# Reordering the opening of an attention and expert kernel: where transposes, scores, the projections of the values and a weight copy stand

## The reference

```python
def xattn(x, y):                                   # x normalized, y = ctx
    q = (x @ Wq + bq).reshape(B, N, 16, 32)
    k = (y @ Wk + bk).reshape(B, 77, 16, 32)
    v = (y @ Wv + bv).reshape(B, 77, 16, 32)
    attn = softmax(einsum('bnhd,bmhd->bhnm', q, k) / sqrt(32))
    out = einsum('bhnm,bmhd->bnhd', attn, v).reshape(B, N, 512)
    return relu(out @ W1 + b1) @ W2 + b2           # 512 -> 1024 -> 512
x = x + xattn(layernorm(x), ctx)
x = x + ffn(layernorm(x))                          # 8 experts, top-1 by layernorm(x) @ Wg.T
```

## Time and profile before

| | |
|---|---|
| median of 3 runs | 1497.59 us (1496.52 to 1498.39) |
| the profiled execution | 1497.29 us |
| its span, first to last instruction | 1495.4 us |
| granted TensorE clock, mean | 0.992 |
| TensorE busy (matmul) | 1462.3 us, 98% |
| VectorE, ScalarE, GpSimd busy | 1028.6, 721.8, 423.4 us |

### The profile page before, as it was taken

The page is one execution under the profiler, slowest core; times in us unless marked ns, Lnnn a source line. Parts: engine busy times, 40 slices in busy tenths (PEclk is TensorE's granted clock), DMA queues, the critical chain, the costliest instruction groups (busy, mean ns, idle before and its releaser), DMA issues.

```text
span 1495.4 us, 23924 instructions
## 1 busy us (share of the span) xinstructions
PE 1462.3 (98%) x7764; PEld 1219.5 (82%) x7764; DVE 1028.6 (69%) x2524; ACT 721.8 (48%) x2026; POOL 423.4 (28%) x312
## 2 busy tenths in 40 slices
PE   7899999999999999999999999999999999999998
PEld 5678787888888888878787888888888878778996
DVE  5666667586868586777767686757585757558665
ACT  5455454453536353635454453536353535434553
POOL 1342121203122222222121203121222222127776
PEclk9899999999999999999999999999999999999999
DMA  7130110213020303131211201120202011649873
GB/s 286 37 101 1 50 36 20 71 44 104 22 99 1 106 15 93 39 84 44 70 51 37 85 22 57 42 89 1 85 1 85 1 57 57 210 172 286 252 236 113
DMA packets 70445, 122.05 MB, mean 82 GB/s; under 512 B 21871, under 2 KB 30336, under 8 KB 69302
## 3 DMA queue, kind: packets, MB, share of 16 engines
q1 hardware_dynamic: 59526, 86.83, 19.4%
q0 software_dynamic: 10800, 33.70, 5.9%
HBM read 75.61 MB, written 46.40 MB: 82 GB/s over the span
## 4 chain that ended last, share of the span: by engine, by line
PE 94%; DVE 3%; ACT 1%; issue 1%; DMA 0%; POOL 0%; POOLq 0%; SPq 0%; DVEq 0%; ACTq 0%
PE bank L1176 24%; PE bank L1198 24%; PE bank L991 11%; PE bank L1128 8%; PE bank L1017 7%; PE bank L1092 4%; PE bank L1600 4%; PE bank L1644 4%; PE bank L1267 2%; PE bank L1583 2%; PE bank L959 2%; PE bank L1245 1%; DVE actH L1109 1%; ACT actH L1103 1%; PE bank L850 1%
## 5 line engine op out<-in xcount | busy, mean ns | idle before, releaser
L1176 PE MATMUL bank<-actA,w 128*128 128x512 f32 x1536 | 373.2, 396 | 2.1 <-issue 2.1
L1198 PE MATMUL bank<-w,actH 128*128 128x512 f32 x1536 | 372.1, 393 | 0.0
L1176 PEld LDWEIGHTS bank<-actA,w 128*128 128x128 f32 x1536 | 285.8, 189 | 64.5 <-issue 2.4
L1198 PEld LDWEIGHTS bank<-w,actH 128*128 128x128 f32 x1536 | 283.0, 188 | 55.9
L1086 POOL TENSOR_TENSOR E<-E,rc 128x1232 f32<-128x1232 f32 x64 | 144.7, 2261 | 460.5 <-DVE rc L1080 460.5
L1342 POOL DMA_INDIRECT region<-rows,pos x64 | 63.8, 997 | 456.4 <-DVE pos L1336 417.9
L991 PE MATMUL bank<-actA,wq 128*128 128x512 f32 x768 | 182.8, 390 | 0.0
L1183 ACT ACTIVATE actH<-bank,b 128x512 fp32r<-128x512 f32 x128 | 88.4, 690 | 190.4 <-PE bank L1176 190.4
L1059 ACT ACTIVATE E<-bank,mx 128x77 f32<-128x77 f32 x512 | 157.6, 359 | 36.6 <-DVE mx L1026 36.6
L991 PEld LDWEIGHTS bank<-actA,wq 128*128 128x128 f32 x768 | 144.6, 189 | 30.7 <-issue 0.7
L1005 DVE SCALAR_TENSOR_TENSOR actQ<-bank,bq,actQ 128x512 fp32r<-128x512 f32 x64 | 48.0, 751 | 163.8 <-ACT actQ L1000 163.8
(11 more groups left out here) (168 smaller groups left out, 2046.1 us busy)
## 6 DMA issues: line engine op xcount, KB each, us to landing
rowB<-region SPq DMA_DIRECT2D x71, 258.0 KB, 3.6
xn<-in_x SPq DMA_DIRECT2D x64, 256.0 KB, 2.9
rows<-in_x SPq DMA_DIRECT2D x64, 256.0 KB, 3.2
w_raw<-in_W SPq DMA_DIRECT2D x2, 2048.0 KB, 13.2
e_raw<-in_E SPq DMA_DIRECT2D x16, 256.0 KB, 2.8
region<-padrow SPq DMA_DIRECT2D x9, 258.0 KB, 2.4
e_parts<-e_high SPq DMA_DIRECT2D x8, 256.0 KB, 2.0
e_parts<-e_low SPq DMA_DIRECT2D x8, 256.0 KB, 2.2
```

The costliest lines, as they stand in the source:

```text
L1176: mm = pe.matmul(p[:], w, a, start=k == 0 and j == 0, stop=k == KD - 1 and j == 2)
L1198: mm = pe.matmul(p[:], a, w, start=m == 0 and j == 0, stop=m == MF - 1 and j == 2)
```

## The change

Only the order of steps of block 0 is changed, no instruction is added or taken away.

- KP 3 stands behind the four row transposes; KLO 0 and 1 stand ahead of them, KLO 2 and 3 behind.
- The key copy, Q 0 and Q 1 come ahead of VP 0; Q 2 comes ahead of the scores, between the two halves of V 0; VLOAD stands behind it.
- Q 3 follows S 0, VP 1 follows S 1, VF 1 follows S 2. VHI 1, CONV_W1 0, VLO 1 and VSTORE 1 come behind all scores.
- CONV_W1 1 moves from the end of the first tail to a place behind OUT(0, 0, A).

The banks are given out by the order of the list, so they change with it.

```diff
--- before.py
+++ after.py
@@ -302,6 +302,8 @@
             step("ADD", b, 0, "A")
             step("ADD", b, 0, "B")
             step("OUT", b, 0, "A")
+            if b == 0:
+                step("CONV_W1", 1)
             for c in CC + CB:
                 step("PT", b, 1, c)
             if b:
@@ -321,7 +323,6 @@
                 for i in (2, 3):
                     step("VF", i)
                     step("VHI", i)
-                step("CONV_W1", 1)
                 for i in (2, 3):
                     step("VLO", i)
                     step("VSTORE", i)
@@ -337,40 +338,42 @@
         step("KP", 1)
         step("CONV_WQ", 0)
         step("KP", 2)
-        step("KP", 3)
+        step("KLO", 0)
+        step("KLO", 1)
         for s in range(SUB):
             step("XT", 0, s)
+        step("KP", 3)
+        step("KLO", 2)
+        step("KLO", 3)
+        step("KSTORE")
+        step("CONV_WQ", 1)
+        step("KCOPY")
+        step("Q", 0, 0)
+        step("Q", 0, 1)
         step("VP", 0)
-        for m in range(KD):
-            step("KLO", m)
-        step("KSTORE")
         step("VF", 0)
         step("VHI", 0)
-        step("CONV_WQ", 1)
+        step("Q", 0, 2)
         step("VLO", 0)
-        step("KCOPY")
         step("VLOAD", 0, 0)
         step("VLOAD", 0, 1)
-        step("Q", 0, 0)
-        step("Q", 0, 1)
         step("MASKS")
         for g in range(KD):
             for s in range(SUB):
                 step("S", 0, g, s)
+            if g == 0:
+                step("Q", 0, 3)
+            if g == 1:
+                step("VP", 1)
+            if g == 2:
+                step("VF", 1)
             step("EXP", 0, g)
             if g:
                 step("SUM", 0, g - 1)
-            if g + 2 < KD:
-                step("Q", 0, g + 2)
-            if g == 0:
-                step("VP", 1)
-            if g == 1:
-                step("VF", 1)
-                step("VHI", 1)
-                step("CONV_W1", 0)
-            if g == 2:
-                step("VLO", 1)
-                step("VSTORE", 1)
+        step("VHI", 1)
+        step("CONV_W1", 0)
+        step("VLO", 1)
+        step("VSTORE", 1)
         step("XLOAD", 0)
 
 
```

## The result

| | median | executions | against before, 95% interval |
|---|---|---|---|
| before | 1497.59 us | 1496.52 to 1498.56 | |
| changed | 1490.99 us | 1488.38 to 1491.52 | 0.9951 [0.9937, 0.9966] |

The kernel is 6.6 us faster by the medians. The profiled execution took 1489.78 us, its span 1487.9; against the profiled one of before (1495.4) that is 7.5 us, since before it lay 0.3 under its median and now it lies 1.2 under it. The forecast was 1492.5, with 5.1 us of gain, in a range of 1489.8 to 1495.7; the band that was given most of the chances, 1491.5 to 1493.5, is missed by 0.5 us on the fast side.

A forecast was written before the change was run, and what follows sets the result against it. TensorE, busy 1147 of 1150 us from 100 to 1250 us, was taken as the bound, so only the beginning was priced. Front 1.7 plus stall 3.4 made 5.1 us: 1492.5 by the median, range 1489.8 to 1495.7.

The forecast's parts named there:

- the front: Reordered steps up to the first attention product (AV): AV at 58.8 instead of 60.5, 1.7 us gained, bounds 0.8 and 3.4.
- the stall: TensorE's 2.05 us wait at L1176 for W1's second part, with half clock behind it: 3.4 us gained, bounds 1.9 and 3.75.
- the first 100 us reach the end whole: Time saved in the first 100 us reaches the end whole, since TensorE is busy at full clock afterwards.
- rival (b): VectorE becomes the second product's bound, three subtractions beside GpSimd costing 1.5 us more: total gain 3.6, 1494.0 us; chance 0.10.
- the lower bound: Stall gain of only 1.9 us, with three of four W2 subtractions beside GpSimd, each up to 0.8 to 1.5 longer.
- The front's lists: Engine queues up to the third GpSimd multiplication: S 1 starts 2.4 us later, the multiplication at 50.2, 1.6 us earlier.
- From the multiplication to AV: Third multiplication at 50.2, transposes at 52.5, VP 2 at 54.45, full clock back at 58.0, AV at 58.8.
- the upper bound of 3.4: Front's largest gain: clock back early enough for VP 2 to take 2.6 us, AV at 57.1.
- (a): Half clock falls on the Q tiles behind new TensorE holes, costing 1.7 us: 1494.2 us; chance 0.13.
- (c): Another wait holds L1176, so the stall and its half clock stay: 1495.9 us; chance 0.04.
- (d): Slower: the first exponentials' 3.9 us delay passes on through the front, 1501.5 us; chance 0.05.
- (e): More gain: the clock does not fall in the softmax, 1490.8 us, or 1490.3 with 3.75 for the stall; chance 0.08.

The follow-up runs named there:

- the repeated timing: The changed kernel timed once more, against executions of the kernel before on the same chip: 1490.24 us, ratio 0.9955.
- e1_w1: Kernel before with only CONV_W1 1 moved behind OUT(0, 0, A): 1493.59 us, ratio 0.9977.
- e3_defer: Kernel before with only VHI 1, CONV_W1 0, VLO 1 and VSTORE 1 put behind all scores: 1493.17 us, ratio 0.9973.
- e4_fill: Kernel before with some last scores and probability transposes repeated in TensorE's holes, results unchanged: 1492.48 us, ratio 0.9971.
- f6_vp2: Changed kernel with VP 2 taken out of the tail and put between the scores of tiles 2 and 3: 1489.72 us, ratio 0.9944.
- f7_late: f6_vp2 with VHI 1 and CONV_W1 0 behind COPY(0, 0), VLO 1 and VSTORE 1 at the tail's end: 1487.21 us; again, 1487.69 us.
- e2_front: Changed kernel with CONV_W1 1 put back at the end of the first tail: 1492.89 us, ratio 0.9970.
- g_xb: Changed kernel with GpSimd's four bias additions of block 0 waiting for all four W2 subtractions of VectorE: one execution, 1493.13 us.
- g_xt: Changed kernel with row transposes behind all four key products and all KLO behind the rows' low halves, as before: 1491.46 us, ratio 0.9956.
- f5_q2: Changed kernel with query tile 2 put back behind the first scores: 1487.36 us, ratio 0.9936.
- Run 4: The same run as e4_fill: kernel before with work repeated in TensorE's holes, 1492.48 us, ratio 0.9971.

## Why the prediction was right, and where it was off

**As a whole.** Sign, range and the split into two parts were right, and the mechanism of each part was. Both terms came out larger than forecast: 4.05 for the front and 3.9 for the stall in the profiles, 7.95 against 5.1; 6.6 us by the medians, 6.7 by the repeated timing's ratio.

**That the first 100 us reach the end whole.** The second product is 7.98 us earlier in the profile, the end 7.5. Right, within what the rest of the kernel varies: from the second product to the end it takes between 1395.7 and 1399.9 us in the profiles here, with no edit there. That is why profiles of one execution and medians differ by 1 us and more.

**The stall.** Forecast 3.4 (1.9 to 3.75); 3.9 in the changed kernel and in e1_w1. The wait, its releaser and the cover of the copy (ScalarE at 60.17, GpSimd at 61.30, both idle) were right. The term was 0.5 short and lies over its upper bound by 0.15, which stays open. 0.35 of it I had given to VectorE's W2 subtractions, but the last one ended at 89.93, just ahead of its user at 90.13. So rival (b) came within 0.2 us. Three of them were slowed beside GpSimd, 1.69, 1.72 and 1.54, as forecast. But before, two of the four ran beside GpSimd, in 1.30 and 2.05 (the earlier trace rows show the 2.05), so that the four together took 6.17 us against 5.80: 0.4 us more, not the 1.5 of the lower bound. In e3_defer, where this stage is not changed, the second product waited 0.36 us until 95.01 (named "issue" as well). The last subtraction had ended at 94.91; that it is the cause was not tried.

**The front's lists.** Step by step: Q 0 forecast at 19.4, measured 19.57; the key copy done at 23.1, 23.3; the first exponential 33.3, 33.45; the maxima of S 1 39.8, 39.75; the third multiplication 50.2, 50.04; the fourth-tile wait for its bank, 45.4, 45.45. Working through what is queued behind what on each engine gave six times within 0.2 us. It also told rightly that most of the moves cancel: S 1 is 2.4 later and its list 2.4 shorter, and what remains is V 1's low half (e3_defer). What it did not see is why S 1 started at 37.43 before: TensorE had been at half clock from 28.9 to 32.3, and VectorE waited 1.53 us for it. An estimate from that wait: with full clock there the old order would have started S 1 some 1.5 us earlier, and the new order would look that much worse against it. e1_w1, e3_defer and e4_fill have this stretch too; no run takes it out of the old order, so this stays open.

**From the multiplication to AV.** This is the term that was mis-sized: 8.6 us forecast (50.2 to 58.8), 6.4 measured. I let the half clock begin where it had begun, and come back 3.5 us behind the start of VP 2. It fell earlier, at 46.4, behind TensorE's hole of 43.7 to 45.4, and was back at 53.2, just before VP 2 began. f6_vp2 and f7_late have VP 2 in that hole, and no half clock in the softmax. So VP 2 took 2.58, not 4.35, and the transposes ahead of it 1.44, not 1.94: 2.3 us more of gain. The front's 4.05 thus lie over even the upper bound of 3.4: that one had VP 2 at 2.6 but left the transposes at 1.94 (0.5 us) and had the multiplication 0.16 later. Five profiles with the reordered front and VP 2 behind it (changed twice, e2_front, g_xb, g_xt) have full clock under VP 2, f5_q2 for two thirds of it; before and e1_w1 have half clock for most of it, e3_defer for its first 2.0 of 3.6 us. Run 4 shows the size: with the clock held up, the old order has VP 2 at 2.58 too. The moment at which the clock comes back was not mine to tell from one profile, and I should have given the upper bound more weight, as the reordering moved the hole ahead of the products and not only the products.

**Rivals.** (a) does occur, in three profiles of ten, and costs what was said; how many of the timed executions hold it is not shown. The Trainium skill (TensorE: Matmul & The Clock Gate, "HAM oscillation — how this bites in real kernels") was right that holes between groups of products bring the clock down, and e3_defer shows that not each of them does: behind its L1176 stall of 2.0 us the clock stayed at 1.00.

```profile
75.80:79.30 3.50, 1.51 (x8) 1.26 (x8) 1.38 (x2) 3.50 (x6) 3.50 (x2) 1.00 0.42 150
```

(b) stayed 0.2 us away. (c) fell by e1_w1. (d) did not happen: the third multiplication came earlier. (e), no half clock at all in the softmax, did not happen, but its price did: 1490.8 forecast, 1490.99 and 1490.24 measured, since VP 2 ran at full clock all the same. (Its second price adds up to 1490.4, not 1490.3.)

## What to carry to other kernels

Where several queues wait for each other, write down for each engine what is queued ahead of the operation that the others need, and count the pieces that leave that list; here taking one 1.50 us operation out of the list brought nearly all that five moves brought there, and one of the moves was a loss of 2 us there. A hole on TensorE can cost a second time, in the clock of what comes behind it, so put independent products into the hole, even repeated ones, rather than on the path. Before a late bound is called covered, look at what else runs on the engine that shares its port.

## What the runs showed of the hardware that I had not expected

- Added work made a kernel faster: 29 matmuls and transposes repeated in holes of TensorE kept the clock at 1.00 instead of 0.50 for 10 us and brought 2.7 us.
- A hole of the same length may or may not bring the clock down. Ahead of the query tiles, 1.7 us did in none of five profiles, 2.18 us in two of four (f6_vp2 and the second f7_late, not the second profile of changed and e2_front), 2.75 us in g_xt did. Ahead of L1176, 2.0 us did in e2_front and e4_fill and not in e3_defer.
- Beside GpSimd's additions (1.26 us each), three of VectorE's 128x4 operations with one SBUF input took 1.22 to 1.30 us instead of 0.17 (g_xb): about as long as one addition, although the operation that waits is tiny.
